# Routed layers of an eight-layer transformer: all experts' split weights kept on chip, 128-slot steps written out on TensorE

## The chip, the cores and the metric

The kernel is one program on one core of a Trainium2 chip. It has five engines that run side by side and wait for one another through semaphores: TensorE (PE, with its weight loads shown apart as PEld), VectorE (DVE), ScalarE (ACT), GpSimd (POOL) and SyncE (SP), which issues most DMAs. Each engine has a sequencer that works through its instruction list in order; rows of the sequencer itself carry a q (PEldq, SPq). The metric is the device time of one execution in microseconds (us); lower is better.

## The reference

Model width D = 512, T = 4 x 512 = 2048 tokens, four pairs of an attention-like layer (`xattn`) and a feed-forward layer (`ffn`), each `x = x + tanh(g) * layer(layernorm(x))`. The change is in the last two feed-forward layers, which route every token to 2 experts out of 8 (inner width 352) and of 16 (inner width 256):

```
# third feed-forward layer ("third"): 8 experts
topk_w, topk_i = top_k(softmax(x @ gate_w.T), 2);  topk_w /= sum(topk_w)
for e in range(8):
    w_e = sum(where(topk_i == e, topk_w, 0))
    out += w_e * ((silu(x @ w_gate[e]) * (x @ w_up[e])) @ w_down[e])

# fourth ("last"): 2 shared experts, which all tokens take, and 16 routed
out = sum_e gelu(x @ Wsh_up[e]) @ Wsh_down[e]
    + sum_e gate_e * (gelu(x @ Wrt_up[e]) @ Wrt_down[e])      # top 2 of 16
```

The context `ctx_1024` (4, 512, 256), of which the first, the third and the fourth `xattn` layer make use, is also touched by the change.

## The kernel before, in words

Every f32 operand of a product is split into two f16 tiles, a high part and the rest (`...h`, `...l`), and a product is three f16 passes: high x high, low x high, high x low. ACT writes the high part, DVE then the low part.

A routed layer (`routed_block`, L468 to L777) runs in three parts. A router block has ranked each token within its expert and given it a place in a list of slots; a step is a stretch of SLOTS = 256 slots that all belong to one expert. There are NS = (2T + E x 255) // 256 steps, that is 23 in the third and 31 in the last layer, whatever the routing; `step_expert` holds the expert of each step and `step_token` the token of each slot.

Then come the steps. In step s:
- SP reads the expert of step s+2 from `step_expert` (L538) and loads that expert's f32 weights into one of two buffers (L540 `mo_up`, L542 and L546 `mo_dn`), then stores the results of step s-1 (L559). The loads wait until DVE has split what stood in the buffer.
- POOL gathers the token rows of step s+2 with two indirect DMAs (L586), once PE has transposed the rows of step s (`mo_g` has two buffers).
- PE transposes the rows of step s+1 (L611, eight 128x128), does the up products of step s (L626: the weights stand still in the array, 256 columns of `mo_y16` move; 72 products in the third layer, 24 in the last), and the down products of step s-1 (L641, 512 columns, 18 and 12 products).
- ACT and DVE split the rows of step s+1, split all weights of step s+1 (ACT L670, L677, DVE L730, L737), and make the middle of step s chunk by chunk (ACT L685 silu or L687 gelu, DVE L744 product, ACT L691 and DVE L747 split); ACT copies the results of step s-1 out of the accumulator (L697).

All engines run the steps as a hardware loop of two steps a turn, so every address on PE is a constant. At the end, 32 times, POOL gathers the two results of 128 tokens (L600, `mo_back`) and ACT, DVE and POOL weight them and add them to `x` (L718, L768, L774).

The split context tiles `ctx_hi` and `ctx_lo` (2 MB each) stay on chip from the first block to the end. The order of the work on each engine is that of the code: no planner moves anything.

Of the kernel before, what the change touches and what calls it, by code (L numbers as in the profile page):

```python
# [103 lines left out]

def setup_block(nc, env):
    env.x = env.keep("x_res", [P, NT, D], F32)
    env.ctx_hi = env.keep("ctx_hi", [P, KC, T], F16)
    env.ctx_lo = env.keep("ctx_lo", [P, KC, T], F16)
# [4 lines left out]
    env.eps5, env.eps6 = env.keep("eps5", [P, 1], F32), env.keep("eps6", [P, 1], F32)  # L113
    ins = env.ins
# [139 lines left out]
SLOTS = 256  # L254
# [3 lines left out]
class Router:  # L258
# [4 lines left out]
    def __init__(self, sb, n_exp, NS):  # L263
# [17 lines left out]
        self.hot_h = sb("hot_h", [P, NT * 2, 2 * NS], F16)  # L281
# [40 lines left out]
    def bases(self, v, c, totals):  # L322
# [4 lines left out]
        c.link(v.tensor_scalar(self.need[:], self.need[:], -ROUND, None, ALU.add))  # L327
# [22 lines left out]
    def spread_tiles(self, v, c, placed):  # L350
        NS = self.NS
        c.link(v.tensor_tensor(self.hot_h[:], self.ramp_pf[:, 0:2 * NS].unsqueeze(1).to_broadcast([P, 2 * NT, 2 * NS]),
                               self.spread(self.tile[:], 2 * NS), ALU.is_equal))
        h4 = self.hot_h[:].rearrange("p (t j) h -> p t (j h)", j=2)
        v.tensor_tensor(h4, h4, self.tokenf[:].unsqueeze(2).to_broadcast([P, NT, 4 * NS]), ALU.mult).then_inc(placed, 1)

    def owners(self, v, c, step_expert, shared):
# [4 lines left out]
        c.link(v.tensor_scalar(self.owner[:], self.owner[:], float(n_exp - 1), float(shared), ALU.min, ALU.add))  # L362
# [3 lines left out]
def router_block(nc, env, y_hi, y_lo, w_router, n_exp, routing, th, down_scale):  # L366
# [6 lines left out]
    with ExitStack() as ctx:  # L373
# [7 lines left out]
        p_token, pl = ps("slot_token", [P, 2 * NS]), ps("logits", [P, NT, n_exp])  # L381
# [7 lines left out]
        @block.sync  # L389
        def _(sp):  # L390
            sp.dma_start(w32[:], w_router.rearrange("(k p) e -> p k e", p=P)).then_inc(w_in, 16)

# [46 lines left out]
        def _(dve):  # L439
# [23 lines left out]
            rt.owners(v, c, step_expert, 0)  # L463
# [4 lines left out]
def routed_block(nc, env, rows, slots_out, w_up, w_down, kind, inner, routing, final):  # L468
# [13 lines left out]
    HS = SLOTS // P  # L482
    passes = [(0, 0), (1, 0), (0, 1)]
    NBK = 5
    with ExitStack() as ctx:
        env.count += 1
        sb, ps = tiles_of(nc, ctx, f"mo{env.count}")
        up32, dn32 = sb("up32", [P, 2, n_up, KD, inner]), sb("dn32", [P, 2, NC, D])
        up16 = [sb(f"up16{h}", [P, 2, n_up, KD, inner], F16) for h in "hl"]
        dn16 = [sb(f"dn16{h}", [P, 2, NC, D], F16) for h in "hl"]  # L490
        cur, g = sb("cur", [P, 2, HS], I32), sb("g", [P, 2, HS, D])
        y16 = [sb(f"y16{h}", [P, 2, KD, SLOTS], F16) for h in "hl"]
        mid = sb("mid", [P, 2, SLOTS])
        sil = sb("sil", [P, 2, SLOTS]) if gated else None
        mid16 = [sb(f"mid16{h}", [P, 2, NC, SLOTS], F16) for h in "hl"]
        o32 = sb("o32", [P, 2, HS, D])
        back = sb("back", [P, NBK, 2, D])
        pT = ps("yT", [P, KD, SLOTS])
        pu = [ps(f"pu{i}", [P, n_up, SLOTS]) for i in range(2)]
        po = [ps(f"po{i}", [P, D]) for i in range(HS)]  # L500
        sem = env.sem
        up_in, dn_in = ([sem(f"{n}{i}") for i in range(2)] for n in ("up_in", "dn_in"))
        g_in, back_in = ([env.dma_sem(f"{n}{i}") for i in range(c)] for n, c in (("rows_in", 2), ("results_in", NBK)))
        up_hi, up_ready, dn_hi, dn_ready = sem("up_hi"), sem("up_split"), sem("dn_hi"), sem("dn_split")
        cur_done, g_go, g_T, yh_done, yl_done = sem("cur"), sem("gather_go"), sem("rows_T"), sem("y_hi"), sem("y_lo")
        up_done, sil_done, mid_done, hi_done, lo_done = (sem("up_done"), sem("silu"), sem("mid"), sem("mid_hi"),
# [6 lines left out]
        def run_steps(engine, step):  # L513

            for s in range(2):
                step(s, s, s < 1, s < 2, False)
# [6 lines left out]
        def turns(s, w):  # L523

            return s + (2 - w)
# [3114 lines left out]
```

## Time and profile before

| | |
|---|---|
| median of 3 runs | 3178.24 us (3177.23 to 3179.23) |
| the profiled execution | 3182.9 us, span in the trace 3181.2 us |
| mean granted TensorE clock | 0.902 of full |
| busy: PE, DVE, ACT, POOL | 2462.9, 2189.4, 1618.2, 1120.6 us |
| steps of the third routed layer | first up product 1787.63 us, first back gather 2098.82 us |
| steps of the last routed layer | 2919.02 us to 3128.32 us |

The rest of the span is the attention and dense layers, the router blocks and the back gathers. A PE row of the timeline groups equal matmuls that follow one another; its time runs to the modelled end of the last one, so the pitch of the instructions is read from one row's start to the next row's start. Of the two levels of TensorE's clock, 1.2 and 2.4 GHz, a stretch with 1.00 had the higher one throughout.

### The profile page before, as it was taken

The numbers are of one execution on the slowest core, as the hardware profiler recorded it, in microseconds if no ns is written. First come the engines' busy times: TensorE is split into PE (matmuls) and PEld (weight loads), VectorE is DVE, ScalarE is ACT, GpSimd is POOL, SyncE is SP. The second block draws the span as 40 slices with busy tenths as digits, with TensorE's granted clock in tenths as the row PEclk, the third lists the DMA queues.
The fourth block names the chain that finished last, engine by engine and source line by source line (L and its number), as shares of the span: only waits on it lengthen the run. The fifth ranks groups of instructions, "written<-read, shape, count | busy, mean of one in ns | idle before, by whom it ended". The sixth has DMA issues, their size and how long they took to land. (4 is left out here: it accounts for less than half of the span.)

```text
span 3181.2 us, 40940 instructions
## 1 busy us (share of the span) xinstructions
PE 2462.9 (77%) x14030; PEld 1173.9 (37%) x14030; DVE 2189.4 (69%) x3435; ACT 1618.2 (51%) x2246; POOL 1120.6 (35%) x807
## 2 busy tenths in 40 slices
PE   2987998899969935676675599937888889797992
PEld 1541332444434301222223477724512222344661
DVE  6656775445456898999996666655588888446664
ACT  2553554154332755555542355535557777433773
POOL 5675766011001235666662222135541000002444
PEclk9987999899979957898896799968989999998996
DMA  3632220220000000000001577743622100313997
GB/s 127 197 152 76 84 84 28 96 86 1 1 4 12 1 0 1 0 0 0 0 0 54 185 241 242 236 132 123 225 103 81 54 15 15 107 41 124 318 298 237
DMA packets 161700, 300.72 MB, mean 95 GB/s; under 512 B 33539, under 2 KB 79375, under 8 KB 159622
## 3 DMA queue, kind: packets, MB, share of 16 engines
q1 hardware_dynamic: 138646, 219.23, 19.8%
q0 software_dynamic: 22896, 79.44, 8.4%
q8 instruction: 92, 1.51, 0.2%
q14 instruction: 66, 0.54, 0.1%
HBM read 206.08 MB, written 92.27 MB: 94 GB/s over the span
## 5 line engine op out<-in xcount | busy, mean ns | idle before, releaser
L1831 DVE TENSOR_REDUCE ac_nmax<-ac_M 128x1 f32<-128x512 f32 (+1 forms) x768 | 492.0, 677 | 93.3 <-PE ac_M L1664 88.9
L1813 ACT ACTIVATE ac_PT<-ac_S 128x1024 f32<-128x1024 f32 x384 | 388.3, 1021 | 205.7 <-PE ac_S L1691 171.2
L3404 POOL TENSOR_TENSOR sc_hc<-sc_h,sc_cs 128x1024 f32<-128x1024 f32 x128 | 300.6, 2355 | 157.1 <-DVE sc_h L3519 101.5
L3519 DVE TENSOR_TENSOR_SCAN sc_h<-sc_dA,sc_dB 128x1024 f32<-128x1024 f32 x128 | 292.1, 2282 | 12.3 <-ACT sc_dA L3485 12.3
L3439 PE MATMUL sc_y<-sc_hc,ident 128*128 128x512 f32 x512 | 257.6, 630 | 18.1 <-DVE x_res L3535 15.8
L3485 ACT ACTIVATE sc_dA<-ss_delta,sc_A 128x511 f32<-128x511 f32 x256 | 166.0, 682 | 29.5 <-DVE sc_h L3519 28.7
L3417 PE MATMUL sc_b<-ss_bc,sc_sel 128*128 128x512 f16 x128 | 54.6, 426 | 152.2 <-DVE sc_dB L3511 120.6
L3490 ACT ACTIVATE sc_cs<-sc_c 128x512 f32<-128x512 f32 x128 | 76.2, 596 | 184.0 <-POOL sc_hc L3404 181.0
L3511 DVE TENSOR_TENSOR sc_dB<-ss_du,sc_b 128x1024 f32<-128x1024 f32 x128 | 156.1, 1220 | 17.7 <-PE sc_b L3417 7.1
L730 DVE SCALAR_TENSOR_TENSOR mo_up16l<-mo_up,mo_up16h 128x1408 f16<-128x1408 f32 (+1 forms) x77 | 112.6, 1464 | 70.4 <-ACT mo_up16h L670 70.3
L1664 PE MATMUL ac_M<-KT,QT 64*128 64x512 f16 (+1 forms) x384 | 135.8, 429 | 31.9 <-DVE ac_nmax L1831 17.2
L3439 PEld LDWEIGHTS sc_y<-sc_hc,ident 128*128 128x128 f32 x512 | 103.0, 203 | 112.4 <-issue 73.6
L626 PE MATMUL mo_pu<-mo_y16h,mo_up16h 128*128 128x256 f16 (+1 forms) x800 | 122.2, 276 | 27.7 <-DVE mo_up16l L730 12.5
L1710 PE MATMUL ac_o<-ac_PT,ac_V 128*32 128x512 f32 x1024 | 138.9, 615 | 0.3 <-ACT ac_oT L1789 0.2
L1664 PE MATMUL ac_M<-ac_KT,ac_QT 64*128 64x512 f16 (+1 forms) x384 | 117.5, 386 | 26.0 <-DVE ac_nmax L1831 19.9
L737 DVE SCALAR_TENSOR_TENSOR mo_dn16l<-mo_dn,mo_dn16h 128x1024 f16<-128x1024 f32 x77 | 79.9, 1063 | 69.2 <-ACT mo_dn16h L677 67.9
L1146 PE MATMUL ap_t<-ident,ap_y 128*128 128x128 f32 x128 | 20.4, 284 | 135.4 <-DVE ap_y L1332 135.4
L626 PE MATMUL mo_pu<-mo_y16l,mo_up16h 128*128 128x256 f16 (+1 forms) x800 | 121.1, 274 | 0.0
L626 PE MATMUL mo_pu<-mo_y16h,mo_up16l 128*128 128x256 f16 (+1 forms) x800 | 120.8, 274 | 0.0
L691 ACT ACTIVATE mo_mid16h<-mo_mid 128x256 f16<-128x256 f32 x131 | 54.6, 417 | 126.2 <-DVE mo_mid L744 119.6
L1691 PE MATMUL ac_S<-QT,KT 64*128 64x512 f16 (+1 forms) x384 | 104.4, 394 | 18.3 <-ACT ac_PT L1813 18.3
L2728 DVE SCALAR_TENSOR_TENSOR f_midl<-f_mid,f_midh 128x512 f16<-128x512 f32 x64 | 54.0, 850 | 83.2 <-ACT f_midh L2661 83.2
(607 smaller groups left out, 6044.9 us busy)
## 6 DMA issues: line engine op xcount, KB each, us to landing
keys_t<-ap_kto SPq DMA_DIRECT2D x32, 512.0 KB, 2.7
queries_t<-ap_qto SPq DMA_DIRECT2D x32, 512.0 KB, 2.7
mo_up<-in_w_gate SPq DMA_DIRECT2D x23, 704.0 KB, 5.2
mo_up<-in_w_up SPq DMA_DIRECT2D x23, 704.0 KB, 6.6
mo_up<-in_exp_up SPq DMA_DIRECT2D x31, 512.0 KB
mo_dn<-in_exp_down SPq DMA_DIRECT2D x31, 512.0 KB
slot_results_last<-mo_o SPq DMA_DIRECT2D x31, 512.0 KB
mo_dn<-in_w_down SPq DMA_DIRECT2D x23, 512.0 KB
```

Source lines behind the costliest of these rows:

```text
L626: last = nc.tensor.matmul(pu[q][0:n, j, :], up16[h][:, w, j, k, c * P:c * P + n], y16[a][:, w, k, :], start=(i == 0), stop=(i == len(passe ...
L730: nc.vector.scalar_tensor_tensor(out=up16[1][:, w, j, :, :], in0=up32[:, w, j, :, :], scalar=SW, in1=up16[0][:, w, j, :, :], op0=ALU.mult, ...
L1664: nc.tensor.matmul(psM[:, slot, :], QT[b % 2][base:base + n, c, j * P:(j + 1) * P], KT[b % 2][base:base + n, :, c, :], start=True, stop=Tr ...
L1691: last = nc.tensor.matmul(psS[:, 2 * (n % 2) + i, :], KT[b % 2][base:base + k, kt, c, :], QT[b % 2][base:base + k, c, :], start=True, stop ...
L1710: last = nc.tensor.matmul(po[r * VC:(r + 1) * VC, :], V[b % 2][:, kt, g % NG * GH + r, :], PT[:, m % PTB, i, :], start=(kt == 0), stop=(kt ...
L1813: nc.scalar.activation(PT[:, n % PTB, :, :], psS[:, 2 * (n % 2):2 * (n % 2) + 2, :], ACT.Exp, scale=SCALE / (SQK * SQK)).then_inc(exp_done, 1)
L1831: last = v.tensor_reduce(out[:, :, 0], sc[:, 0:MAIN], AX.X, ALU.max)
L3404: nc.gpsimd.tensor_tensor(hc[:, m % RC, :, :], h[:, m % RH, :, :], cs[:, m % 2, :].unsqueeze(1).to_broadcast([P, W, S]), ALU.mult).then_in ...
L3439: last = nc.tensor.matmul(py[:, c, :], env.id32[:], hc[:, m % RC, c, :], start=(n == 0), stop=(n == NS - 1))
L3485: last = nc.scalar.activation(dA[:, m % 2, c, 1:S], delta[:, b * KD + k, 1:S], ACT.Exp, scale=A[:, k, n:n + 1])
L3511: nc.vector.tensor_tensor(dB[:, m % RB, :, :], chans(du, b, p), pb[:].unsqueeze(1).to_broadcast([P, W, S]), ALU.mult).then_inc(dB_done, 1)
L3519: nc.vector.tensor_tensor_scan(h[:, m % RH, :, :].rearrange("p c s -> p (c s)"), dA[:, m % 2, :, :].rearrange("p c s -> p (c s)"), dB[:, m ...
```

## The change

The number of slots in a step goes from 256 to 128, so there are NS = (2T + E x 127) // 128 = 39 and 47 steps. Each expert now has one step at least (`need` is at least 1), so step s < E belongs to an expert numbered s or lower. The split f16 weights of all experts of the layer stay on chip (`up16`, `dn16` have an expert axis). A new class `Arriving` brings each expert's f32 weights once, piece by piece (gate, up, down; or up, down), through a ring of NST = 3 stage tiles; the first three pieces are loaded in the router block. During the first E steps ("filling"), ACT and DVE split the pieces of expert s+1.

PE's steps are written out (no loop). The roles in the up product are changed over: the rows stand still, and the weights move, 352 or 256 columns; the result has the tokens on the partitions, so the middle has to be transposed before the down product (L692 with 3 or 2 transposes). PE loads the expert of the next step from `step_expert` (L667) and addresses the weights through that register. Per step PE has 4 transposes, 24 up, 3 transposes, 9 down products in the third layer, and 4, 12, 2 and 6 in the last.

The context tiles are given back after the third `xattn` layer: the first one stores them to DRAM in 8 DMAs, the fourth loads them again.

```diff
-SLOTS = 256
+SLOTS = 128
...
+            for q in range(arriving.NST):
+                arriving.load(sp, q)
...
+class Arriving:
...
+    def load(self, sp, q):
+        e, i = divmod(q, self.NPC)
...
+        for a, b in zip(self.views(e, i), src):
+            sp.dma_start(a, b).then_inc(self.sems[q % self.NST], 16)
...
+        up16 = [sb(f"up16{h}", [P, n_exp, n_up, KD, inner], F16) for h in "hl"]
+        dn16 = [sb(f"dn16{h}", [P, n_exp, NC, D], F16) for h in "hl"]
...
         def _(sp):
+            def load(e, i):
+                q = e * NPC + i
+                if q >= NST:
+                    sp.wait_ge(w_ready, arriving.split(q - NST))
+                    arriving.load(sp, q)
...
+            def step(s, w):
+                if filling(s) and s + 2 < n_exp:
+                    load(s + 2, 0)
+                if from_step(s, 2):
+                    store(s - 2, w)
+                if filling(s) and s + 2 < n_exp:
+                    for i in range(1, NPC):
+                        load(s + 2, i)
...
+            def down(s, w, e):
+                if filling(s):
+                    pe.wait_ge(w_ready, arriving.split(s * NPC + n_up))
+                if from_step(s, 2):
+                    pe.wait_ge(o_done, s - 1)
+                pe.wait_ge(lo_done, s + 1)
+                i = 0
+                for c, n in enumerate(chunks):
+                    for a, b in passes:
+                        last = nc.tensor.matmul(po[w][:], mid16[a][0:n, w, c, :], dn16[b][0:n, bass.ds(e, 1), c, :],
+                                                start=(i == 0), stop=(i == len(passes) * NC - 1))
...
+            for s in range(NS):
+                w = s % 2
+                if s + 1 < NS:
+                    rows_transposed(s + 1, 1 - w)
+                if filling(s):
+                    pe.wait_ge(w_ready, arriving.split(s * NPC + n_up - 1))
                 pe.wait_ge(yl_done, s + 1)
...
+                up(s, w, e, (0,))
+                if s:
+                    middle_transposed(s - 1, 1 - w)
+                up(s, w, e, (1, 2))
+                if s:
+                    down(s - 1, 1 - w, before)
+                if s + 1 < NS:
+                    e, before = expert_of(s + 1), e
...
+            def step(s, w):
+                more = filling(s) and s + 1 < n_exp
+                if from_step(s, 2):
+                    results(s - 2, w)
+                if before_end(s, 1):
+                    y_high(s + 1, 1 - w)
+                if from_step(s, 1):
+                    middle_high(s - 1, 1 - w)
+                if more:
+                    weights_high(s + 1, (0,))
+                first_half(s, w)
+                if more:
+                    weights_high(s + 1, range(1, NPC))
```

On PE, in the third routed layer, the start of a step in the hardware loop of before stands so (`mo_yT` is the transposed rows, `mo_pu` and `mo_po` the accumulators of the up and down products; an ISA row is a small instruction of the sequencer, here a wait):

```order
L606 ISA
L608 ISA
L611 MATMUL mo_yT<-ident,mo_g 128x128 x8
L615 ISA
L616 ISA
L621 ISA
L626 MATMUL mo_pu<-mo_y16h,mo_up16h 128x256 x4
L626 MATMUL mo_pu<-mo_y16l,mo_up16h 128x256 x4
L626 MATMUL mo_pu<-mo_y16h,mo_up16l 128x256 x4
L626 MATMUL mo_pu<-mo_y16h,mo_up16h 128x256 x4
```

And so in the changed kernel, where the step begins with the load of the expert's number:

```order
L704 MATMUL mo_po<-mo_dn16l,mo_mid16h 128x512
L667 TENSOR_LOAD step_expert_third
L667 ISA x2
L674 MATMUL mo_yT<-ident,mo_g 128x128 x4
L682 ISA
L682 MATMUL mo_pu<-mo_up16h,mo_y16h 128x352
L682 ISA
L682 MATMUL mo_pu<-mo_up16h,mo_y16h 128x352
```

Between every two products there is now an ISA row, which computes the address of the moving operand; the rows of a group of four equal products no longer stand together. Further on in the same step the transposes of the middle stand between the first up pass and the second (`mo_midT` is the transposed middle of the step before):

```order
L682 ISA
L682 MATMUL mo_pu<-mo_up16h,mo_y16h 128x352
L692 MATMUL mo_midT<-ident,mo_mid 128x128 x3
L682 ISA
L682 MATMUL mo_pu<-mo_up16h,mo_y16l 128x352
```

These three transposes are what is new there; before, the up product's result already had the inner width on the partitions. On SP, from the end of the router block into the third routed layer, this stands before:

```order
L391 DMA rt_w<-in_gate_w_t 128x4x8
L373 UNCONDITIONAL_BRANCH
L530 UNCONDITIONAL_BRANCH
L538 TENSOR_LOAD step_expert_third
L538 ISA x2
L540 ISA
L540 DMA mo_up<-in_w_gate 128x4x352
L540 ISA
L540 DMA mo_up<-in_w_up 128x4x352
L542 ISA
L542 DMA mo_dn<-in_w_down 128x2x512
```

And this in the changed kernel:

```order
L396 DMA rt_w<-in_gate_w_t 128x4x8
L514 DMA arriving_third<-in_w_gate 128x4x352
L514 DMA arriving_third<-in_w_up 128x4x352
L514 DMA arriving_third<-in_w_down 128x2x512
L514 DMA arriving_third<-in_w_down 96x512
L378 UNCONDITIONAL_BRANCH
L596 UNCONDITIONAL_BRANCH
L514 DMA arriving_third<-in_w_gate 128x4x352
```

The three pieces of the first expert are issued ahead of the branch out of the router block, and the read of `step_expert` is gone from SP.

## Rows read from the trace of the kernel before

**Rows 1.** Windows: stretch, busy us of each engine (instructions), PEclk, DMA share, GB/s.
```profile
1820.00:1840.00 20.00, 19.46 (x144) 14.34 (x143) 12.91 (x17) 10.88 (x20) 3.30 (x4) 1.00 0.78 265
3000.00:3020.00 20.00, 19.33 (x136) 13.43 (x135) 12.87 (x16) 15.83 (x28) 7.77 (x10) 1.00 1.00 345
```

**Rows 2.** Timeline of PE, third layer: start, us, operation, [idle before <-releaser].
```profile
1838.35 1.04 PE L611 MATMUL mo_yT<-ident,mo_g 128*128 128x128 f32 x8
...
1847.81 0.38 PE L641 MATMUL mo_po<-mo_dn16h,mo_mid16h 128*128 128x512 f16 x1
...
1851.71 1.04 PE L611 MATMUL mo_yT<-ident,mo_g 128*128 128x128 f32 x8
```

**Rows 3.** Timeline of PE, last layer, one step.
```profile
2929.99 1.04 PE L611 MATMUL mo_yT<-ident,mo_g 128*128 128x128 f32 x8
2930.86 0.60 PE L626 MATMUL mo_pu<-mo_y16h,mo_up16h 128*128 128x256 f16 x4
2931.30 0.60 PE L626 MATMUL mo_pu<-mo_y16l,mo_up16h 128*128 128x256 f16 x4
...
2936.07 0.71 PE L611 MATMUL mo_yT<-ident,mo_g 128*128 128x128 f32 x5
```

**Rows 4.** Groups by form, both routed layers: count | busy, mean ns | idle before, releaser.
```profile
L730 DVE SCALAR_TENSOR_TENSOR mo_up16l<-mo_up,mo_up16h 128x1408 f16<-128x1408 f32 x46 | 74.7, 1625 | 37.1 <-ACT mo_up16h L670 37.0
L670 ACT ACTIVATE mo_up16h<-mo_up 128x1408 f16<-128x1408 f32 x46 | 62.5, 1360 | 0.0
...
L670 ACT ACTIVATE mo_up16h<-mo_up 128x1024 f16<-128x1024 f32 x31 | 32.6, 1053 | 30.6 <-DMA mo_up<-in_exp_up 28.3 <-issue 1.8 <-PE mo_pu L626 0.4
...
L730 DVE SCALAR_TENSOR_TENSOR mo_up16l<-mo_up,mo_up16h 128x1024 f16<-128x1024 f32 x31 | 38.0, 1225 | 33.3 <-ACT mo_up16h L670 33.2
...
L747 DVE SCALAR_TENSOR_TENSOR mo_mid16l<-mo_mid,mo_mid16h 128x256 f16<-128x256 f32 x62 | 25.9, 417 | 1.3 <-ACT mo_mid16h L691 1.3
```

**Rows 5.** Sequencer rows by line: count: ns min/median/max, first and last start.
```profile
L621 PEldq FUSED_REGOPS  x2: 42/46/51, 1839.0 to 1839.9; - x2
...
L608 PEldq FUSED_REGOPS  x1: 42/42/42, 1847.9 to 1847.9; - x1
...
L538 SPq FUSED_REGOPS  x98: 16/152/192, 1771.9 to 3108.4; - x98
...
L538 SPq TENSOR_LOAD <-step_expert_third x23: 262/277/486, 1771.4 to 2057.6; - x23
```

**Rows 6.** Timeline at both ends of the third layer's steps.
```profile
1779.99 1.97 PE L611 MATMUL mo_yT<-ident,mo_g 128*128 128x128 f32 x8 [9.54 <-DMA mo_g<-normalised,mo_cur]
...
1787.63 1.01 PE L626 MATMUL mo_pu<-mo_y16h,mo_up16h 128*128 128x256 f16 x4 [1.26 <-DVE mo_up16l L730]
...
2095.05 0.60 ACT L697 ACTIVATE mo_o<-mo_po 128x512 f32<-128x512 f32 x1 [1.29 <-PE mo_po L641]
...
2098.82 0.94 POOL L600 DMA_INDIRECT mo_back<-slot_results,slot_third  x1 [55.62 <-SPq L569]
```

**Rows 7.** DMA issues of the page: KB each, us from issue to landing.
```profile
mo_up<-in_w_gate SPq DMA_DIRECT2D x23, 704.0 KB, 5.2
```

**Rows 8.** The tile `mo_up`: all its loads in both routed layers.
```profile
DMA to landing us min/median/max: 4.2/6.2/11.6
```

**Rows 9.** Timeline: both ends of the last layer's steps; a 512-column split.
```profile
2171.64 0.69 DVE L1337 SCALAR_TENSOR_TENSOR ap_yl<-ap_t,ap_yh 128x512 f16<-128x512 f32 x1 [1.38 <-ACT ap_yh L1266]
...
2912.86 1.97 PE L611 MATMUL mo_yT<-ident,mo_g 128*128 128x128 f32 x8 [13.21 <-DMA mo_g<-normalised_last,mo_cur]
...
2919.02 1.06 PE L626 MATMUL mo_pu<-mo_y16h,mo_up16h 128*128 128x256 f16 x4
...
3128.32 0.95 POOL L600 DMA_INDIRECT mo_back<-slot_results_last,slot_last  x1 [27.29 <-SPq L569]
```

**Rows 10.** Windows of the third `xattn` layer, columns as in rows 1.
```profile
1250.00:1270.00 20.00, 12.78 (x34) 4.59 (x33) 19.38 (x13) 11.37 (x18) 13.06 (x6) 1.00 0.00 1
1450.00:1470.00 20.00, 9.95 (x24) 4.12 (x23) 16.06 (x12) 12.81 (x18) 9.34 (x5) 0.67 0.00 0
```

## What I predicted before the changed kernel ran

> **What bounds the kernel now.** I read the page first (busy shares, slices, the chain), then windows inside both routed layers, then PE's timeline over one step of each, the groups by form there, the sequencers' rows, and the edges of both stages. Only the two routed layers change by more than a microsecond or two, so the question is what ends last in each.
>
> In the third layer's loop PE is busy 19.46 of 20 us [rows 1]. One step runs from 1838.35 to 1851.71, that is 13.36 us [rows 2]. The array's pitches: 18 down products from 1847.81 to 1851.71 are 0.217 us each at 512 columns [rows 2]; eight transposes take 0.87 us (0.109 each) and four 256-column products 0.44 (0.109 each) [rows 3]. So 72 x 0.109 + 18 x 0.217 + 8 x 0.109 = 12.6 of the 13.36 us: this layer is bound by PE, at 6.68 us per 128 slots. In the last layer one step is 6.08 us (2929.99 to 2936.07) [rows 3], which is 24 x 0.109 + 12 x 0.217 + 0.87 = 6.09: also PE. But from 2919.02 to the first back gather at 3128.32 [rows 9] there are 209 us, less 8.6 us of tail; 31 steps make 6.45 each, since the loads run at 345 GB/s with a DMA share of 1.00 [rows 1] and ACT waits 28.3 us in all for `mo_up` [rows 4]. So here PE and the DMA take turns.
>
> **The change: padding.** 23 x 256 = 5888 slots become 39 x 128 = 4992 (15% less); 31 x 256 = 7936 become 47 x 128 = 6016 (24% less). The work per slot decides the rest.
>
> **Third layer, a steady step.** 24 products of 352 columns: between 0.109 at 256 and 0.217 at 512 a straight line gives 0.149, together 3.58 us. 9 x 0.217 = 1.95, 7 transposes x 0.109 = 0.76. Sum 6.29 us, against 6.68 before for the same slots. Waits on the middle's chain (silu, product, transposes, split) lie beside 16 up products (2.4 us); I take 6.4 us.
>
> **The register.** Each up and down product now has an address computation ahead of it on PE's sequencer, and each step a load of the expert's number. No row of before has PE do this. From below: PE's small register instructions take 42 to 65 ns by the rows of L621 and L608 (42, 46 and 51) [rows 5]; a plain load-and-multiply pair costs the sequencer about 0.03 us (24 of them lie between the two rows of L621 at 1839.0 and 1839.9, less the wait) [rows 5]: 0.08 us together. From above: SP's address instructions have a median of 152 and a maximum of 192 ns [rows 5]: 0.18 to 0.22 us. I take 0.14, near the middle, since the work is SP's and the engine is PE. The number's load: 0.28 us on SP [rows 5] and two register instructions, 0.65 us with latency. Third layer: 33 x 0.14 + 0.65 + about 0.3 = 5.6 us, under the array's 6.29, so hidden. Its cover is the sequencer's lead: the row of L608 at 1847.9 stands 3.8 us before its transposes at 1851.71 [rows 2, 5].
>
> The Trainium skill, "DMA: Bandwidth & Descriptors", section on latency and other measured facts, gives a floor of about 600 ns for a `tensor_load`. SP's rows here have a median of 277 ns, and by these I go; by the page the 86 loads would weigh 0.3 us more each, nothing in the third layer and up to 10 us in the last, where the sequencer has little lead.
>
> **Third layer, filling.** Steps 0 to 7 can't outrun the weights. A stage tile goes round in landing + ACT + DVE: 5.2 us [rows 7] + 1.36 + 1.62 [rows 4] = 8.2 us, and three tiles carry just one expert's three pieces. The transfer alone: 2.7 MB (weights, results, rows) at 345 GB/s [rows 1] is 7.8 us. I take 8.4. First up product: before at 1787.63, after transposes that waited for rows until 1779.99 [rows 6]; these rows were in line with 4 MB of weights, and the rest of the delay is the split of weights. With the pieces of expert 0 loaded beside the router I expect about 1782.3. So up(7) at 1782.3 + 7 x 8.4 = 1841; then 31 steps x 6.4 give 2040 for up(38), and a tail of 12 us (rest of the step, transposes, down, results, store, of which the last 3.8 us from result to back gather are as before [rows 6]). Back gather at about 2052 instead of 2098.8: **-47 us**. Before minus after checks as 23 x 13.36 = 307 against 7 x 8.4 + 32 x 6.4 = 264, and 5 us at the start.
>
> **Last layer.** First up product at 2912 instead of 2919.0: its rows arrived at 2912.86 behind the weights [rows 9]. Filling: three tiles carry one and a half experts, so (5.2 + 1.05 + 1.23 [rows 4, 7]) x 2/3 = 5.0 us; the DMA floor is 1.57 MB at 345 GB/s = 4.6; I take 5.1, x 15 = 77 us, up(15) at 2989. Steady step: the array needs 12 x 0.109 + 6 x 0.217 + 6 x 0.109 = 3.26 us. The sequencer needs 18 x 0.14 + 0.65 + 0.3 = 3.5. And the chain bites: after the middle's transposes come ACT's split (about 0.42) and DVE's (0.417 for 256 columns [rows 4]; a 512-column one takes 0.69 [rows 9]), with two semaphores, before the down product, against a cover of 8 products of 0.14; then the wait stands on the sequencer's own instruction, so its lead is gone and the next number's load follows. I take 4.0 us; 31 x 4.0 = 124; tail 8.6: 3121.6 instead of 3128.3: **-7 us**. 24% less slots, but per slot 4.0 against 6.45 / 2 = 3.2.
>
> **The rest.** Router: two DVE operations on 1472 columns shrink: -1 us. Context out and in again: 4 MB beside the weights blocks of both `xattn` layers, hidden, 0 to +2. The context's space is what pays for resident weights. Back gathers: paced by POOL, unchanged; their four buffers instead of five I cost at nothing. Other blocks keep their instructions.
>
> **Sum.** 3182.9 - 47 - 7 - 1 + 1 = 3129 us on the basis of the profiled execution, which lay 4.7 us above the median; on the median's basis **3124 us**.
>
> **Bounds.** Steady steps: third 6.29 to 6.7 (-3 to +10 us); last 3.5 to 4.4 (-15 to +12). Filling: landing from 4.2 (the least) or 5.2 to 6.2 us (the median of all loads) [rows 8]: the third +1 x 7, the last +0.7 x 15, some +17; the DMA floors -10. The start of either layer may bring nothing (+5 and +7). Together, as independent terms, 3100 to 3150.
>
> **Rival A: the sequencer becomes the bound; no change or slower.** At 0.22 us for a register-addressed product the third layer's step is 33 x 0.22 + 0.95 = 8.2 us and the last's 18 x 0.22 + 0.95 = 4.9: + 31 x 1.8 + 31 x 0.9 = +84, so about 3208 us, slower than before. The point from which it decides: at 0.20 us the steps are 7.55 and 4.55, +53 us, which is the whole gain. At 0.17 the third layer still hides all but little (6.6). For it: SP's 152 to 192 ns for the same kind of work. Against: PE's own register rows of 42 to 65 ns. Chance 0.20 with its milder half (0.18 to 0.21, around 3160 to 3185), of which 0.12 on the slower side. The Trainium skill, "TensorE: Matmul & The Clock Gate", section on what happens when a matmul is issued, says that without hardware decode the sequencer spends about 62 ns per product; the plain pairs here go at 0.03 us, so that path is not taken now, and should a register operand lead into it, it would mean 0.03 us more than my 0.14, which by itself leaves the third layer where it is.
>
> **Rival B: the clock falls while the stages fill.** In a filling step PE has 6.3 of 8.4 us of work (75%), in the last layer 3.26 of 5.1 (64%). A stretch with 64% busy shows a clock of 1.00, one with 50% shows 0.67 [rows 10]. At 1.2 GHz all through, the array would need 12.6 and 6.5 us: +4.2 x 7 + 1.4 x 15 = +50, about 3175 us. Chance 0.07, for part of it already in my range.
>
> **Rival C: the last layer runs free.** If the register costs 0.10 and the chain is covered, the last layer's step is 3.4 and its filling 4.7: -19 - 6, so 3099 us. Speaks for it: the 0.08 end. Against: the wait on the sequencer is there at any price of the register. Chance 0.20.
>
> **Rival D: landings stretch.** The ring holds three pieces, and the results' stores and the row gathers share the engines. At 7 us landing: 10 and 6.3 us per filling step: +11 + 18, about 3153. Chance 0.13; the loads' maximum of 11.6 us speaks for it [rows 8], the median against.
>
> **How the numbers follow.** My forecast (3100 to 3150) has 0.40, C 0.20, D 0.13, B 0.07, A 0.20. The range reaches down into C (3092) and up to D, B and the milder half of A (3180). A measurement can tell 0.2% (6.4 us) from no change: below 3171.8 is faster, above 3184.6 slower. Faster 0.81, within 0.06, slower 0.13.
>
> **What would show it.** Right: PE's step in the third layer at 6.3 to 6.5 us with a busy share near 1; filling steps with PE waiting for `mo_up16l`/`mo_dn16l` from DVE and these for landings; back gather at 2045 to 2060. In the last layer about 4.0 us with PE's idle time ahead of the first down product put down to `mo_mid16l`, and ahead of the transposes to nothing (the sequencer). Wrong: 352-column products at a pitch over 0.16 us everywhere (the register), a PEclk of 0.5 to 0.7 in filling, or a filling step over 9.5 us. What would make it wrong altogether is a product pitch of 0.2 us or more in both layers.

## The result and the profile after

The changed kernel takes 3138.9 us (median of 4 runs, 3137.9 to 3140.2) against 3177.7 before: a ratio of 0.9878 (95% interval 0.9861 to 0.9895), or 39 us less. The forecast was 3124, 54 less. The profiled execution took 3137.9 us (span 3136.1), 45 us less than the profiled one of before.

Windows of the changed kernel: filling and steady steps of the third layer, then of the last (columns as in rows 1; to be read against [rows 1]).

```profile
1781.00:1849.00 68.00, 47.49 (x272) 28.73 (x272) 45.98 (x49) 41.93 (x54) 15.78 (x15) 0.94 0.87 270
1849.00:2043.00 194.00, 194.00 (x1234) 124.77 (x1233) 56.63 (x95) 64.32 (x125) 32.32 (x57) 1.00 0.25 82
2868.00:2946.00 78.00, 56.05 (x352) 34.98 (x351) 49.86 (x59) 52.06 (x87) 25.30 (x30) 0.98 0.89 293
2946.00:3075.00 129.00, 113.36 (x743) 72.60 (x743) 32.95 (x64) 61.74 (x126) 34.32 (x58) 1.00 0.39 123
```

In the third layer's steady steps PE has no gap at all, and the DMA engines are at a quarter. While a layer fills, PE has 70% and 72% of work and the DMA engines 87% and 89%. In the last layer's steady steps 12% of PE's time is idle although the DMA share has fallen to 0.39: something else is late there.

Timeline of PE, changed kernel, third layer (start, us, operation, [idle before <-releaser]): the first transposes and up product, and two steady steps. They answer to [rows 2, 6].

```profile
1775.25 1.08 PE L674 MATMUL mo_yT<-ident,mo_g 128*128 128x128 f32 x4 [5.46 <-DMA mo_g<-normalised,mo_cur]
...
1781.58 2.53 PE L682 MATMUL mo_pu<-mo_up16h,mo_y16h 128*128 x8 [2.64 <-DVE mo_up16l L805]
1783.89 2.04 PE L682 MATMUL mo_pu<-mo_up16h,mo_y16l 128*128 x8
1785.77 1.36 PE L682 MATMUL mo_pu<-mo_up16l,mo_y16h 128*128 x8
...
1792.70 2.53 PE L682 MATMUL mo_pu<-mo_up16h,mo_y16h 128*128 x8 [5.14 <-DVE mo_up16l L805]
...
1854.82 1.36 PE L682 MATMUL mo_pu<-mo_up16h,mo_y16h 128*128 x8
...
1861.11 1.36 PE L682 MATMUL mo_pu<-mo_up16h,mo_y16h 128*128 x8
```

The steady pitch is 6.29 us, to the hundredth what the sum of array times gave. At the start of each of the first two filling steps eight products take 2.3 us instead of 1.2. The clock is at its lower level there, as windows of these stretches show (columns as above):

```profile
1781.00:1786.00 5.00, 4.42 (x18) 2.45 (x19) 3.11 (x5) 2.18 (x3) 1.27 (x1) 0.57 0.87 249
1792.00:1796.00 4.00, 3.29 (x14) 2.20 (x15) 2.83 (x4) 2.26 (x4) 0.00 (x0) 0.57 0.83 255
```

Ahead of the first stretch PE had been busy for 6.9 of 34 us (1741 to 1775, beside the router), and right ahead of the second it had waited 5.14 us for a weight split. The end of the third layer's steps, from POOL's timeline, answers to [rows 6]; the start of the back gathers in the last layer to [rows 9]:

```profile
2056.23 0.94 POOL L661 DMA_INDIRECT arriving_third<-slot_results,slot_third  x1 [29.31 <-SPq L627]
...
3084.91 0.95 POOL L661 DMA_INDIRECT arriving_last<-slot_results_last,slot_last  x1 [19.98 <-SPq L627]
```

The terms, forecast against the profiled execution (step starts are those of the first up pass; U7 at 1848.45, U38 at 2043.08; last layer U0 at 2867.81, U15 at 2946.26, U46 at 3074.64):

| term, us | forecast | measured |
|---|---|---|
| third: first up product | 1782.3 | 1781.6 |
| third: 7 filling steps | 58.8 | 66.9 |
| third: 31 steady steps | 198.4 | 194.6 |
| third: tail to the back gather | 12 | 13.2 |
| from there to the last layer's first up product | 813.2 | 811.6 |
| last: 15 filling steps | 76.5 | 78.5 |
| last: 31 steady steps | 124 | 128.4 |
| last: tail | 8.6 | 10.3 |

Differences to the kernel before: up to the back gather of the third layer -42.6 us; from there to the last layer's first up product 811.6 us against 820.2, -8.6 (of which 0.4 before the fourth `xattn`'s first transposes); last layer from first up product to back gather 217.1 against 209.3, +7.8; the end -1.7. Sum -45.1.

One steady step of the last layer in the changed kernel, timeline of PE, ACT and DVE in that order:

```profile
2996.17 0.63 PE L674 MATMUL mo_yT<-ident,mo_g 128*128 128x128 f32 x4
...
2997.07 0.38 PE L692 MATMUL mo_midT<-ident,mo_mid 128*128 128x128 f32 x2
...
2998.82 0.39 PE L704 MATMUL mo_po<-mo_dn16h,mo_mid16h 128*128 x1 [0.38 <-DVE mo_mid16l L816]
...
3000.32 0.63 PE L674 MATMUL mo_yT<-ident,mo_g 128*128 128x128 f32 x4
```
```profile
2996.91 0.60 ACT L739 ACTIVATE mo_y16h<-mo_yT 128x512 f16<-128x512 f32 x1
2997.57 0.39 ACT L761 ACTIVATE mo_mid16h<-mo_midT 128x256 f16<-128x256 f32 x1
```
```profile
2997.54 0.69 DVE L796 SCALAR_TENSOR_TENSOR mo_y16l<-mo_yT,mo_y16h 128x512 f16<-128x512 f32 x1 [3.07 <-ACT mo_y16h L739]
2998.15 0.42 DVE L816 SCALAR_TENSOR_TENSOR mo_mid16l<-mo_midT,mo_mid16h 128x256 f16<-128x256 f32 x1
```

Here `y_high` and `y_low` are ACT's and DVE's splits of the next step's rows, `middle_high` and `middle_low` those of the middle. Read it as one round: transposes 2996.17, ACT's `y_high` 2996.91, DVE's `y_low` 2997.54, only then `middle_low` 2998.15, down products 2998.82, and the transposes again at 3000.32. The down products wait behind a split of rows which only the next step needs: `middle_high` is done at 2997.96, and DVE starts `middle_low` 0.2 us later. From the middle's transposes at 2997.07 to the first down product are 1.75 us. The sequencer's rows of the round after it (count: ns min/median/max, first and last start):

```profile
L667 PEldq FUSED_REGOPS  x2: 151/151/151, 2999.9 to 3004.0; - x2
...
L667 PEldq TENSOR_LOAD <-step_expert_last x1: 295/295/295, 3003.7 to 3003.7; - x1
```
```profile
L704 PEldq FUSED_REGOPS  x6: 46/53/60, 3002.9 to 3003.5; - x6
...
L682 PEldq FUSED_REGOPS  x6: 51/55/55, 3001.4 to 3002.1; - x6
```

The starts of six address computations lie 0.66 us apart from the first to the last at the up products (3001.43 to 3002.10) and 0.69 at the down products (3002.86 to 3003.55), so 0.13 to 0.14 us each: the register costs 0.10 us over a plain pair of 0.03. The number's load and its register instruction take from 3003.7 to about 3004.2; in the round of the step shown above the transposes stand 0.2 us behind the last down product's slot (2999.90 + 0.22).

### The profile page after: what moved, and what is told of

Same layout as the page of the kernel before. It is cut to its first block and busy times, and to the rows that moved or that the text cites. A ratio compares the mean times of both kernels' runs of the same rounds, so it can differ in the third digit from the quotient of the medians.

```text
span 3136.1 us, 39908 instructions
## 1 busy us (share of the span) xinstructions
PE 2396.2 (76%) x13100; PEld 1076.3 (34%) x13100; DVE 2056.3 (66%) x3302; ACT 1503.3 (48%) x2076; POOL 1081.3 (34%) x818
## 5 line engine op out<-in xcount | busy, mean ns | idle before, releaser
L796 DVE SCALAR_TENSOR_TENSOR mo_y16l<-mo_yT,mo_y16h 128x512 f16<-128x512 f32 x86 | 59.3, 689 | 169.7 <-ACT mo_y16h L739 169.7
L704 PE MATMUL mo_po<-mo_dn16h,mo_mid16h 128*128 (+1 forms) x211 | 80.5, 381 | 37.9 <-DVE mo_mid16l L816 37.7
L640 POOL COPY mo_cur<-step_token_last 128x1 int32 (+1 forms) x47 | 11.8, 251 | 281.0 <-POOLq L72 177.6
L1676 POOL TENSOR_TENSOR ac_psum<-ac_PT 128x1024 f32<-128x1024 f32 x32 | 74.8, 2361 | 81.3 <-PE ac_M L1820 81.2
L682 PE MATMUL mo_pu<-mo_up16h,mo_y16h 128*128 x500 | 84.8, 305 | 20.9 <-DVE mo_up16l L805 20.6
L1776 PE MATMUL ac_S<-ac_QT,ac_KT 64*128 64x512 f16 (+1 forms) x384 | 98.9, 383 | 2.0 <-ACT ac_PT L1898 1.9
```

The costliest lines, as they stand in the source:

```text
L682: last = nc.tensor.matmul(pu[w][:, j, 0:inner], y16[a][:, w, k, :], up16[h][:, bass.ds(e, 1), j, k, :], start=(i == 0 and k == 0), stop=(i ...
L704: last = nc.tensor.matmul(po[w][:], mid16[a][0:n, w, c, :], dn16[b][0:n, bass.ds(e, 1), c, :], start=(i == 0), stop=(i == len(passes) * NC ...
L1776: last = nc.tensor.matmul(psS[:, 2 * (n % 2) + i, :], KT[b % 2][base:base + k, kt, c, :], QT[b % 2][base:base + k, c, :], start=True, stop ...
```

## Experiments

In these rounds the kernel before took 3179.4 to 3180.4 us, 2 to 3 more than the 3177.7 beside the changed kernel, which was not timed again. A difference between an experiment and the changed kernel's 3138.9 is therefore good to some 3 us; the steps and stages are read from the traces.

**Constant experts on PE.** Is it the round or the sequencer?

```diff
-                return pe.value_load(step_expert[0:1, s:s + 1], min_val=0, max_val=n_exp - 1)
+                return s % n_exp
...
-                            last = nc.tensor.matmul(pu[w][:, j, 0:inner], y16[a][:, w, k, :], up16[h][:, bass.ds(e, 1), j, k, :],
+                            last = nc.tensor.matmul(pu[w][:, j, 0:inner], y16[a][:, w, k, :], up16[h][:, e, j, k, :],
...
```

> PE takes the weights of expert s modulo the number of experts, a constant of the program, in place of the routed one; no number is loaded and no address computed on PE (the output is that of a wrong routing). The order of all else is that of the changed kernel. Theory 1 (the last layer's steady step of 4.14 us is a round through transposes, y_high, y_low, middle_low and down products; the sequencer adds only what its load of the number keeps the transposes waiting): step 3.95 us, the layer 6 us shorter, third layer's step unchanged at 6.29, total about 3133. Theory 2 (the sequencer's work on 18 register-addressed products and the load sets the step): step 3.3 to 3.5 us, total about 3115.

3124.7 us; the last layer's steady step 3.83 us ((3061.06 - 2942.45) / 31), between the two forecasts; the third layer's 6.31, unchanged. The down products still wait for `mo_mid16l`, by PE's timeline of this kernel:

```profile
2949.26 0.38 PE L704 MATMUL mo_po<-mo_dn16h,mo_mid16h 128*128 128x512 f16 x1 [0.39 <-DVE mo_mid16l L816]
...
2953.07 0.38 PE L704 MATMUL mo_po<-mo_dn16h,mo_mid16h 128*128 128x512 f16 x1 [0.39 <-DVE mo_mid16l L816]
```

So the round holds most of the step, and load and register together 0.31 us of 4.14, where theory 1 had given the load 0.19. Of the 14 us in the total 10 lie in these steps; the rest are a start 1.5 us earlier, a filling of the third layer 1.8 us shorter, and 2.3 us between the layers.

**Middle before rows on ACT and DVE.** The diff shows ACT; DVE's `middle_low` and `y_low` change places likewise.

```diff
-                if before_end(s, 1):
-                    y_high(s + 1, 1 - w)
                 if from_step(s, 1):
                     middle_high(s - 1, 1 - w)
+                if before_end(s, 1):
+                    y_high(s + 1, 1 - w)
```

> One order changed in both layers: ACT splits the middle of step s-1 ahead of the rows of step s+1, and DVE likewise. Theory 1 (a round through y_high, y_low, middle_low): the down products no longer wait for a split that only the next step needs; last layer's step 4.14 to 3.7 us, -13 us, total about 3126; third layer unchanged at 6.29. Theory 2 (sequencer): step stays at 4.1, total 3139.

3134.3 us, step 4.00: right in its direction, a third of the size (0.14 us in place of 0.44). Timeline of PE, then DVE, in one step of this kernel:

```profile
3001.17 0.38 PE L692 MATMUL mo_midT<-ident,mo_mid 128*128 128x128 f32 x2
...
3002.76 0.39 PE L704 MATMUL mo_po<-mo_dn16h,mo_mid16h 128*128 x1 [0.26 <-DVE mo_mid16l L816]
```
```profile
3002.09 0.42 DVE L816 SCALAR_TENSOR_TENSOR mo_mid16l<-mo_midT,mo_mid16h 128x256 f16<-128x256 f32 x1 [2.79 <-ACT mo_mid16h L761]
3002.57 0.69 DVE L796 SCALAR_TENSOR_TENSOR mo_y16l<-mo_yT,mo_y16h 128x512 f16<-128x512 f32 x1
```

The next wait had stood right behind the first: transposes, split and split of the middle alone take 1.59 us (3001.17 to 3002.76) beside eight products of 0.11, hardly less than the 1.75 before.

**Next number loaded before the down products.**

```diff
+                after = expert_of(s + 1) if s + 1 < NS else None
                 if s:
                     down(s - 1, 1 - w, before)
-                if s + 1 < NS:
-                    e, before = expert_of(s + 1), e
+                if after is not None:
+                    e, before = after, e
```

> PE loads the number of the next step's expert ahead of the down products of step s-1 in place of behind them, so that the load's 0.6 us lie beside up products and the wait for the middle. Theory 1 (round through the splits): only the 0.15 us between the last down product and the transposes go, step 4.0 us, total about 3134. Theory 2 (sequencer): the load's whole time goes from the step, 3.6 us, total about 3122.

3136.3 us, last layer's step 3.95, 0.19 less: the gap behind the down products is gone and nothing more, as theory 1 has it.

**All three orders**: the two above, and the middle's transposes ahead of all 12 up products (the diff shows only these):

```diff
+                if s:
+                    middle_transposed(s - 1, 1 - w)
...
-                up(s, w, e, (0,))
-                if s:
-                    middle_transposed(s - 1, 1 - w)
-                up(s, w, e, (1, 2))
+                up(s, w, e, (0, 1, 2))
```

> Three orders changed: ACT and DVE split the middle ahead of the rows, PE loads the next number ahead of the down products, and PE transposes the middle ahead of the first up pass in place of behind it. Reading of the runs so far: with the rows' splits out of the way the down products still wait for transposes, split and split of the middle (1.59 us from the transposes' start to the first down product, beside 8 products of 0.11), so the last layer's step only fell to 4.0. With all 12 up products beside that chain: step 3.4 to 3.5 us in place of 4.14, about -21 us; third layer unchanged at 6.3; total about 3118. Rival (PE's sequencer with 18 address computations and the load sets about 3.9): total about 3131.

3121.1 us; last layer's step 3.65 ((3058.62 - 2945.49) / 31), 0.2 over the forecast. **The same with constant experts:**

> The same order, with constant experts on PE: no number loaded, no address computed (a wrong routing). If the chain of the splits was what made the register's cost show, the step is the same as with registers within 0.1 us, total within 4 us of it. If the sequencer is the bound there, the step is 0.3 us or more shorter (-10 us or more).

3106.5 us; step 3.28, which is the array's own sum of 3.26. The rival was right here: with the round out of the way the load and the register cost 0.37 us a step. PE's timeline of the kernel with registers shows where, then its sequencer:

```profile
3001.62 0.60 PE L682 MATMUL mo_pu<-mo_up16l,mo_y16h 128*128 x4
3002.32 0.39 PE L704 MATMUL mo_po<-mo_dn16h,mo_mid16h 128*128 x1
3002.62 0.39 PE L704 MATMUL mo_po<-mo_dn16h,mo_mid16l 128*128 x1
3002.84 0.38 PE L704 MATMUL mo_po<-mo_dn16l,mo_mid16h 128*128 x1
```
```profile
L667 PEldq TENSOR_LOAD <-step_expert_last x1: 303/303/303, 3001.5 to 3001.5; - x1
L667 PEldq FUSED_REGOPS  x1: 151/151/151, 3001.8 to 3001.8; - x1
```

The up products end at 3002.06 by their pitch; the first down product starts at 3002.32, behind the load that began at 3001.5, and the second 0.30 us after it instead of 0.22. These two gaps, 0.26 and 0.08, are nearly all of the 0.37. Twelve address computations at 0.13 us against 0.11 us of array leave the sequencer no lead to hide the load in. In the third layer 352 columns (0.15 us) do: its step is 6.33 us with registers and 6.30 with constants.

**Two stage tiles in both layers** (the ring's size 3 becomes 2):

> The ring has two stage tiles in place of three, in both layers (two pieces loaded in the router). Theory A (a filling step is set by a tile's way round: landing, ACT, DVE, about 8.2 us third, 7.5 last): third 3/2 x 8.2 = 12.3 us per expert in place of 9.6, +19 us; last 7.5 in place of 5.2, +34 us; total about 3192. Theory B (set by what the DMA engines move, 2.7 and 1.57 MB at 300 to 345 GB/s): under +10 us, total about 3147.

3186.3 us, ratio 1.0019 (1.0010 to 1.0029) to the kernel before: the whole gain gone. Filling: third 83.8 us (12.0 per expert, forecast 12.3), last 101.3 (6.75, forecast 7.5). PE is busy for 55 of the third's 83 us, at a granted clock of 0.81, so it doesn't set the pace. Theory A, with one thing that it had not said: with fewer loads in flight each lands sooner. The loads of the third layer's gate and up pieces, first in the changed kernel, then here (KB each, median us from issue to landing):

```profile
arriving_third<-in_w_gate SPq DMA_DIRECT2D x7, 704.0 KB, 6.0
arriving_third<-in_w_up SPq DMA_DIRECT2D x7, 704.0 KB, 6.7
```
```profile
arriving_third<-in_w_up SPq DMA_DIRECT2D x7, 704.0 KB, 4.3
arriving_third<-in_w_gate SPq DMA_DIRECT2D x6, 704.0 KB, 4.7
```

**Five stage tiles in the last layer**, the context tiles closed behind the projection so that they fit:

```diff
+                if rope:
+                    context_tiles(nc, env, "last")
                 attention_weights_block(nc, env, w, rope)
                 attention_project_block(nc, env, w, rope)
+                if rope:
+                    env.context.close()
...
-    env.arriving = Arriving(nc, env, env.late, "last", [env.ins["exp_up"]], env.ins["exp_down"], 256, SHARED, 3)
+    env.arriving = Arriving(nc, env, env.late, "last", [env.ins["exp_up"]], env.ins["exp_down"], 256, SHARED, 5)
```

> Five stage tiles in the last layer (third layer as it is); the context tiles of the fourth xattn layer are given back ahead of its core so that they fit. Theory A: the filling step of the last layer falls from 5.23 to the transfer's 4.6 to 4.7 us, 8 us less, and two more pieces come beside the router; total about 3130. Theory B (transfer or the order of ACT's splits bounds already): filling 5.1 to 5.2, total 3137 to 3139.

3124.1 us; filling 65.6 us (4.38 per expert) in place of 78.5, 13 of the 15 us. Window of its filling:

```profile
2870.00:2935.00 65.00, 53.51 (x350) 34.44 (x349) 50.25 (x59) 53.20 (x87) 21.68 (x30) 0.99 0.97 334
```

DMA share 0.97 at 334 GB/s against 0.89 at 293: now the transfer bounds it. At 4.38 us per expert it takes less than the 4.6 of my floor, since five of the 32 pieces are issued beside the router in place of three; by size and rate (2 x 0.52 MB at 334 GB/s) I estimate 3 of the 13 us for these two.

**Weights of expert 0 split before its rows.** The diff shows ACT; DVE's two calls change places likewise.

```diff
-            y_high(0, 0)
             weights_high(0, range(NPC))
+            y_high(0, 0)
```

> The changed kernel; ACT and DVE split expert 0's weights, which have landed long before, ahead of the first rows in place of behind them. In the trace of the changed kernel ACT waited for the first rows until 1776.4 with the weights there. Expected: first up product of the third layer 3 to 4 us earlier, and since the ring's tiles come free 5 to 6 us earlier, its filling 2 to 3 us shorter; last layer 2 to 3 us and 2 us; total -10 us, about 3129. Rival: the first loads then meet the rows' gathers and delay them, no gain, 3139.

3133.8 us. Third layer: first up product at 1780.9, only 0.7 us earlier; filling 61.9 us, 5 less. PE's timeline of this kernel:

```profile
1775.48 1.11 PE L674 MATMUL mo_yT<-ident,mo_g 128*128 128x128 f32 x4 [6.51 <-POOL mo_mid L652]
1780.00 1.12 PE L674 MATMUL mo_yT<-ident,mo_g 128*128 128x128 f32 x4 [3.41 <-DMA mo_g<-normalised,mo_cur]
1780.91 2.55 PE L682 MATMUL mo_pu<-mo_up16h,mo_y16h 128*128 x8
```

The rows of step 1, whose transposes stand ahead of step 0's up products, are now what PE waits for, until 1780.0. The freed tiles filled earlier all the same. In the last layer the filling took 77.2 us, 1.3 less. The gain is half of the 10 us expected.

**Weights not loaded beside the router.**

> The first three pieces of weights are issued in the routed block in place of the router, in both layers. Theory A (the early loads are what brings the first up product forward): third layer's first up product 5 us later, last layer's 4 us later, total about 3148. Theory B (the rows alone set the start, which smaller gathers bring): within 2 us, about 3140.

3148.1 us. Third layer's first up product at 1786.4, 4.8 us later than in the changed kernel; the last layer's stands 816.0 us behind the third's back gathers instead of 811.6. Both starts are as theory A has them. That the total came out at its 3148 is partly luck: the third layer's filling was 2.6 us shorter in this execution and its steady steps 4.4 us longer in all (199.0 against 194.6 us). In those PE had 2.6 us of gaps and the clock was at its lower level for 3.4 us, which theory A says nothing of; what brought the gaps stays open.

**The kernel before with 128-slot steps alone** (SLOTS = 128, the wait for a step's rows counting one gather).

> The kernel before with steps of 128 slots alone: 39 and 47 steps, weights loaded and split at each step as before, up products with 128 moving columns. Theory 1 (the smaller steps pay only with resident weights): third layer 1.9 MB of weights a step and splits of about 7.5 us on DVE, step about 7.8 us, 39 of them 304 us, as before; last layer bound by 1.6 MB a step, 5.5 to 6 us x 47 = 270 against 200, so total about 3245, slower than before. Theory 2 (less padding is the whole gain): third layer 39 x 6.7, last 47 x 4.2, total about 3130.

3370.5 us, ratio 1.0599 (1.0582 to 1.0617), far slower than my 3245: a step of the third layer takes 11.6 us, not 7.8. A window, PE's transposes of two steps in a row, then the timeline (DVE and ACT) in one of them:

```profile
1900.00:1940.00 40.00, 27.57 (x295) 23.29 (x296) 25.00 (x39) 22.23 (x42) 3.55 (x7) 0.85 0.71 230
```
```profile
1908.89 0.60 PE L611 MATMUL mo_yT<-ident,mo_g 128*128 128x128 f32 x4
...
1920.51 0.60 PE L611 MATMUL mo_yT<-ident,mo_g 128*128 128x128 f32 x4
```
```profile
1909.41 1.36 ACT L670 ACTIVATE mo_up16h<-mo_up 128x1408 f16<-128x1408 f32 x1
...
1910.80 1.62 DVE L730 SCALAR_TENSOR_TENSOR mo_up16l<-mo_up,mo_up16h 128x1408 f16<-128x1408 f32 x1 [0.97 <-ACT mo_up16h L670]
...
1912.34 0.28 DVE L744 SCALAR_TENSOR_TENSOR mo_mid<-mo_pu,mo_sil 96x128 f32<-96x128 f32 x1
...
1912.74 0.31 ACT L691 ACTIVATE mo_mid16h<-mo_mid 96x128 f16<-96x128 f32 x1 [1.81 <-DVE mo_mid L744]
```

No engine is full: PE 69%, DVE 63%, ACT 56%, DMA 0.71. As the timeline reads, ACT and DVE take turns (ACT waits for `mo_mid`, which stands behind DVE's weight split, which waits for ACT), a round that depends on the weights and hardly on the slots. With 256 slots it lay beside 12.6 us of PE. No run took this round apart, so it is a reading and not shown. Small steps without resident weights lose 191 us, 141 of them in the third layer's steps (452.0 us from first up product to back gather against 311.2).

**The context to DRAM and back, in the kernel before.**

> The kernel before, with the context stored to DRAM in the first xattn layer and loaded again in the fourth, as in the changed kernel, and nothing else. If both lie beside the weights blocks, as the trace of the changed kernel reads: 0 to +2 us against before. The rival that they cost what their queue shows, 5.6 us in the fourth layer's weights block and as much in the first: +5 to +10.

3179.6 us, ratio 0.9997 (0.9987 to 1.0006): nothing, although SP's queue was held 6.1 us by the first load of the context. Its first transposes of the fourth `xattn` layer start at 2169.86, to the hundredth as in the trace of before. This execution (span 3178.0) also shows something of the sum's basis: its last layer's steps ran from 2918.20 to 3125.26, 207.1 us, against 209.3 in [rows 9], by the same instructions there.

**All that helped together**: the three orders, expert 0's weights first, five stage tiles in the last layer.

> The three orders of the steady step, the weights of expert 0 split first, and five stage tiles in the last layer. If the gains add: -21 - 10 - 15 = -46 us, about 3093 us, a ratio of 0.973 to the kernel before; since a faster ring and an earlier start share part of one gain, 3090 to 3103.

3105.6 us, ratio 0.9768 (0.9752 to 0.9784), the fastest of those that take the routed experts: 74 us under before, 33 under the changed kernel. It stayed short of the sum of the single gains (18 + 5 + 15 = 38 us under the changed kernel). Its filling of the last layer takes 64.8 us, hardly less than the 65.6 with five tiles alone, so the earlier start bought nothing more there. In its trace the third layer's first up product stands at 1782.8, not earlier than in the changed kernel (1781.6), and the way between the two layers takes 814.2 us against 811.6; why is open.

## Why the prediction was right, and where it was off

- *What bounds it, padding and residency.* Right. PE was the bound of the third layer's step and still is, at 6.29 us for 128 slots. The smaller step alone costs 191 us, so the gain needs resident weights. The other half, resident weights with 256-slot steps, was not run. From the rows of before I estimate that it could take at most 17 us out of the third layer (23 steps, 13.36 against 12.6 us of array) and 11 out of the last (31 steps, 6.45 against 6.09), so part of the 39 us may be residency alone. Nor did a run take apart the exchanged roles in the up product.
- *Third layer's steady step.* 6.4 was put down, 6.29 is what the terms gave and what came. The 0.1 for waits was not needed. That these steps came out 3.8 us shorter than forecast and offset half of what the filling cost was luck.
- *Register (0.14 us per product, hidden in the third layer).* Measured 0.13, and hidden there (6.31 us with constant experts). The 0.14 was the middle between two bounds, and that it came so near is luck: the address instruction itself takes 0.051 to 0.055 us, like PE's own register rows (which run from 42 to 51 ns in [rows 5], not to 65) and a third of SP's, and no row of before showed the rest. The number's load was sized right: 0.65 us from its start to the next instruction. In the last layer load and register weren't covered: 0.31 us per step, 10 us in all. Rival A, in which it would bound both layers, did not come about.
- *Filling.* The mechanism (a tile's way round) was right, as two and five tiles show; the term was mis-sized in the third layer by 8 us: 9.55 us per expert against 8.4, just over the 9.5 that I had named as a sign of being wrong. Followed piece by piece from issue, landing and split rows, the 18 pieces from the third expert on take 5.8 us to land on the mean (5.2 was put down), then 0.35 until ACT takes them up, since ACT splits in a fixed order and behind waits for the step's own work (nothing was put down), then 1.44 and 1.69 for the two splits (1.36 and 1.62); with the waits between them 9.4 against 8.2. Landings of these loads in the changed kernel:

```profile
DMA to landing us min/median/max: 3.8/5.6/8.5
```

  The first step, at the lower clock and with expert 1's first piece only issued at 1779.9, took 11.1.
- *Last layer.* This is the step that failed: -7 us was forecast, and -8.6 + 7.8 = -0.8 came. The start came as worked out, but steady steps at 4.14 instead of 4.0 (+4.4), filling +2.0 and tail +1.7 took it back. The prediction had seen the chain through the middle's splits and the load, and missed that DVE's `y_low` stands ahead of `middle_low`; with the middle first the step is the 4.00 that was forecast. In the filling, landings of 5.5 us on the mean in place of 5.2 account for the 2.0. Nothing was run on the tail.
- *Basis.* Of the 15 us between forecast and median, 9 are these terms; of the other 6 the profiled execution of before, which lay 5 above its median, makes 5, and that of the changed kernel, which lay 1 below its own, makes 1. I took the difference over unchanged, as if all 5 lay outside the layers that change. The second execution of nearly the same instructions had 2.2 us less in the last layer's steps, so part of it lay inside, where the DMA bounds; where the rest lies stays open.
- *Context, router.* Nothing and about -1, as forecast: POOL's first copy behind the third layer's router starts at 1770.61 in place of 1771.28, and DVE's work at the end of the last one is 0.4 us shorter.
- *Rivals and range.* Rival B (clock) showed only in the first steps of each filling: PEclk 0.94 and 0.98 over all of it. Rival C's step of 3.4 is not reached even with better orders (3.65). Rival D was half right for the third layer: its filling step of 10 us lay nearer to 9.55 than my 8.4 did, its landing of 7 us did not come (5.8), and the last layer's 6.3 stayed away (5.23). The prediction also says that its range reaches from 3092 to 3180, into the rivals; the range that it states, 3100 to 3150, doesn't.

## What to carry to other kernels

When an order of work is written out, look on every engine for what stands ahead of the instruction that the bound engine waits for, and ask who needs it and when; then look for the next wait behind it, because the first edit may give back only a third (0.14 of the 0.49 us that all three orders gave here) until the second is made as well. A register operand on TensorE was free here where the array took 0.15 us per product, against the sequencer's 0.13, and showed where it took 0.11. For data that pass a ring once, count landing plus every engine's turn, divided by the tiles, and take the landing from a stretch with as many loads in flight: here two tiles more were worth 13 us in one layer, and one tile less cost the whole gain.

## What the runs showed of the hardware

A product with a register-addressed moving operand costs PE's sequencer 0.13 us against 0.03 for a plain one, of which the address instruction is 0.053; SP's address instructions of 0.152 were no guide to it. The load of a number from a tile takes PE's sequencer 0.30 us, its register instruction 0.151; in the kernel with all three orders the next instruction stands 0.65 us behind the start of the load (3001.46 to 3002.11), an assertion of 0.018 us among them. The Trainium skill, "DMA: Bandwidth & Descriptors", section on latency and other measured facts, gives about 600 ns as the floor of a `tensor_load`; the trace agrees if all of this is meant, and has half of it for the load itself. Landings in the third layer's filling, at a DMA share of 0.87, spread from 3.8 to 8.5 us, and the 704 KB ones took 6.0 and 6.7 us at the median with three tiles in the ring, 4.3 and 4.7 with two.
